# Causal layer: two projection jobs a batch, with the even and the odd features of all heads side by side in a bank

## The chip, the cores and the metric

The kernel runs on one core of a Trainium2 chip, in one launch. The metric is the device time of that core in microseconds (us). A core has five engines with a queue each: PE multiplies matrices, DVE (vector) and ACT (scalar) work on tiles, POOL (GpSimd) works on tiles in SBUF, and SP issues most DMAs here. PE writes its results to PSUM banks (512 floats per partition each); DVE and ACT read them there.

## The reference, cut to what matters

Two decoder layers run over x (16 batches, 256 rows, 256 features). The change touches the first sub-layer alone: causal self-attention with 16 heads of 16 features and a rotary embedding of q and k.

```
x = x + L0_attn(layernorm(x))                  # changed here; then cross attention,
                                               # a product-key FFN, band attention, a bidirectional
                                               # attention and a mixture of experts
L0_attn: k, q, v = split(x @ W_KQV.T, 3)       # 16 heads x 16 features
  rope:  xr, xi = x[..., ::2], x[..., 1::2]    # even and odd features of a head
         yr = xr*cos - xi*sin
         yi = xr*sin + xi*cos
  out = softmax(causal(rope(q) @ rope(k).T / 4)) @ v, then @ W_O.T
```

## The kernel before, in words

`attention_stage` is used three times (kinds causal, cross, band). The causal one works on 16 batches. `program` has a short lead-in (norm, turn, project and values for batches 0 and 1) and then calls `macro(e, b, par)` for each batch b. A macro is a list of 16 steps s, one per head, and every engine's queue is filled by walking the same list, so the order of work on an engine is the order of the calls in `macro`. At each step the engines handle three batches at once: `head(b, s)` computes the scores of batch b that go into the exponential, `find(b + 1, s)` computes scores of batch b + 1 whose row maximum DVE takes, and at chosen steps the work of batch b + 2 (`turn`, `project`, `stack`) and the end of batch b - 1 (`weigh`, `sums`, `sums_end`, `normalise`, `out`) is put in.

- `project(b + 2, j)` is a projection job. On PE it multiplies the transposed, normalised x with weights into bank (j + 1) % 2 of `ps_p`; the causal layer has weights wq and wk and copies of them with the two features of each pair swapped (wqs, wks), so that one bank holds q and its swapped form side by side. DVE multiplies the two halves with the cosine and sine tables into `rot`, and adds them twice, into `full` (float32) and into `part` (bfloat16). POOL then makes two more bfloat16 parts (middle and low) out of the remainder, with three instructions. SP writes the parts to DRAM scratch tensors (`qscratch`, `kscratch`), and `stack` reads them back, rearranged by head, into `qs` and `ks`.
- `find(h)` uses bank h % 2 of `ps_1`. PE may only write it when the maximum of head h - 2 has been taken, so it waits for `nmax_ready` to count h - 1 heads. DVE takes the two maxima of a head (row halves) with two TENSOR_REDUCE.
- `head(h)` uses `ps_2` in the same way with ACT's exponential (`p_ready`).
- `sums` and `sums_end` are two DVE reciprocals of 128 columns each; `normalise` on PE waits for the second of them (`rr_ready`). `norm(b + 3)` on DVE (s = 4) is two TENSOR_SCALAR from SBUF to SBUF. `moments` (s = 3) is two BN_STATS.
- `out(b - 1)` at s = 13 waits on PE for `proj_used` of all jobs of batch b + 2, because it writes bank 0 of `ps_p`.

In a table of what matters, the steps are these before the change:

| step s | calls that matter, in their order |
|---|---|
| 1 | turn |
| 2 | weigh (last quad of b - 1), project j = 0 |
| 3 | moments |
| 4 | sums, norm |
| 5 | sums_end, project j = 1 |
| 6 | weigh |
| 7 | normalise |
| 8 | stack, project j = 2 |
| 9 | turn_max |
| 10 | weigh |
| 11 | project j = 3 |
| 13, 15 | out; values |

The last call of each step (before turn_max) is `find(b + 1, s)`, and the first is `head(b, s)`.

## Time and profile before

| | us |
|---|---|
| median of 3 runs | 3635.33 (3632.45 to 3639.7) |
| the profiled execution's own time | 3634.44 |
| its span, first to last instruction | 3632.6 |

| engine | busy us over the span | share |
|---|---|---|
| PE | 3238.9 | 89% |
| DVE | 2620.0 | 72% |
| POOL | 2067.8 | 57% |
| ACT | 1834.9 | 51% |

The causal stage is the first 515.8 us or so: its last instruction on DVE (L880) starts at 515.1. In it the 16 macros run from about 67 to 515 us, and from the second to the fourteenth they repeat every 28.5 us. Busy shares are averages over stages with different limits, so what the change is worth is read from one macro.

### The profile page before, as it was taken

What the parts mean: (1) busy time and instruction counts of PE and PEld (TensorE: products, weight loads), DVE (VectorE), ACT (ScalarE), POOL (GpSimd) and SP (SyncE); (2) the same over time, 40 slices, a digit from 0 to 9 for tenths busy, and PEclk for the clock granted to TensorE, in tenths of its full rate; (3) what the DMA queues carried; (4) which work ended last, traced back from release to release, by engine and by line L of the source; (5) the groups of instructions that cost most, each with busy time, mean ns of one, the idle gap of its engine ahead of it and who ended that gap; (6) DMA issues with size and microseconds to landing.
All of it is one profiled execution on the core that took longest, in us unless ns stands there. A gap on an engine that the chain in (4) does not pass through costs nothing. (4 is left out here: it accounts for less than half of the span.)

```text
span 3632.6 us, 95157 instructions
## 1 busy us (share of the span) xinstructions
PE 3238.9 (89%) x33694; PEld 2753.6 (76%) x33695; DVE 2620.0 (72%) x10695; ACT 1834.9 (51%) x4800; POOL 2067.8 (57%) x2454
## 2 busy tenths in 40 slices
PE   5999977876599999999999999978888898899998
PEld 4777754554589999999999999855555686899998
DVE  6666634453899999999999999848888577333333
ACT  1434434543577777777777777726565221222221
POOL 4444435552377777777777777758886232333332
PEclk8999988997799999999999999989999898899999
DMA  5444424442200000000000000035553231566665
GB/s 155 111 118 125 109 66 119 122 116 74 84 2 2 2 2 2 2 2 2 3 2 2 2 3 2 2 82 128 138 131 88 84 100 44 170 185 177 186 176 134
DMA packets 255744, 277.73 MB, mean 76 GB/s; under 512 B 43871, under 2 KB 200287, under 8 KB 254815
## 3 DMA queue, kind: packets, MB, share of 16 engines
q1 hardware_dynamic: 241694, 253.40, 24.1%
q0 software_dynamic: 13632, 18.91, 3.6%
q8 instruction: 245, 4.01, 0.5%
q14 instruction: 173, 1.41, 0.1%
HBM read 187.34 MB, written 72.29 MB: 71 GB/s over the span
## 5 line engine op out<-in xcount | busy, mean ns | idle before, releaser
L1295 POOL TENSOR_TENSOR peer_hot_v<-peer_hot_e,peer_parts 80x512 bf16<-80x512 bf16 x768 | 920.9, 1226 | 271.0 <-DVE peer_hot_e L1338 266.2
L1091 PE MATMUL peer_ps_u<-peer_up,peer_g 128*128 128x256 f32 x2048 | 513.8, 396 | 0.6 <-DVE x_all L1438 0.6
L1072 PEld LDWEIGHTS peer_ps_h<-peer_xnT,peer_down 128*128 128x128 f32 x4096 | 503.9, 195 | 13.6 <-DMA peer_down<-in_peer_down 1.0
L1072 PE MATMUL peer_ps_h<-peer_xnT,peer_down 128*128 128x128 f32 x4096 | 505.9, 278 | 0.7 <-DMA peer_down<-in_peer_down 0.7
L1201 ACT ACTIVATE peer_hot_u<-peer_count,peer_minus_u 80x128 bf16<-80x128 bf16 x1536 | 462.3, 426 | 2.6 <-PE peer_ps_w L1082 1.5
L1082 PE MATMUL peer_ps_w<-peer_hot_v,peer_hot_u 80*128 80x32 bf16 x12288 | 348.3, 177 | 80.9 <-DVE peer_g L1352 36.1
L1091 PEld LDWEIGHTS peer_ps_u<-peer_up,peer_g 128*128 128x128 f32 x2048 | 382.5, 197 | 49.5 <-issue 1.0
L1082 PEld LDWEIGHTS peer_ps_w<-peer_hot_v,peer_hot_u 80*128 80x128 bf16 x12288 | 338.1, 97 | 101.2 <-issue 64.6
L2272 POOL DMA_INDIRECT out<-moe_y,moe_target x71 | 112.5, 1585 | 312.6 <-DVE moe_y L2371 309.6
L1169 ACT ACTIVATE peer_g<-peer_ps_h 128x512 f32<-128x512 f32 x256 | 145.3, 590 | 249.4 <-PE peer_ps_h L1072 249.1
L2216 PE MATMUL moe_ps_t<-moe_xgT,moe_w 128*128 128x128 f32 x2272 | 267.9, 277 | 0.0
L2216 PEld LDWEIGHTS moe_ps_t<-moe_xgT,moe_w 128*128 128x128 f32 x2272 | 262.0, 194 | 0.1
L2226 PE MATMUL moe_ps_y<-route_w,moe_hT 128*128 x1136 | 256.8, 379 | 0.0
L2226 PEld LDWEIGHTS moe_ps_y<-route_w,moe_hT 128*128 128x128 f32 x1136 | 210.5, 190 | 25.7
L1344 DVE TENSOR_TENSOR peer_hot_u<-peer_count,peer_uvT 80x2048 bf16<-80x2048 bf16 x160 | 229.9, 1437 | 0.0
L707 ACT ACTIVATE causal_probT<-causal_ps 128x384 f32<-128x384 f32 x256 | 124.5, 488 | 204.3 <-PE causal_ps L611 201.3
L2252 ACT ACTIVATE moe_hT<-moe_hT 128x512 f32<-128x512 f32 x142 | 89.4, 629 | 229.4 <-DVE moe_hT L2362 229.4
L843 DVE TENSOR_REDUCE band_nmax<-band_ps 128x2 f32<-128x512 f32 x256 | 171.6, 680 | 41.9 <-PE band_ps L584 41.3
L840 DVE TENSOR_REDUCE causal_nmax<-causal_ps 128x1 f32<-128x128 f32 (+1 forms) x512 | 153.0, 349 | 58.2 <-PE causal_ps L588 57.8
L1206 ACT ACTIVATE peer_hot_u<-peer_hot_u,peer_iota 80x2048 bf16<-80x2048 bf16 x96 | 192.2, 2002 | 3.1
L1352 DVE TENSOR_TENSOR peer_g<-peer_ps_w,peer_g 128x512 f32<-128x512 f32 x256 | 173.9, 679 | 11.8 <-PE peer_ps_w L1082 11.8
L707 ACT ACTIVATE band_probT<-band_ps 128x512 f32<-128x512 f32 x256 | 146.9, 593 | 64.2 <-PE band_ps L608 59.9
(373 smaller groups left out, 7235.0 us busy)
## 6 DMA issues: line engine op xcount, KB each, us to landing
moe_w<-in_moe_w SPq DMA_DIRECT2D x142, 512.0 KB, 4.5
causal_qs<-causal_qscratch SPq DMA_DIRECT2D x32, 384.0 KB, 3.9
cross_qs<-cross_qscratch SPq DMA_DIRECT2D x32, 384.0 KB, 3.6
band_qs<-band_qscratch SPq DMA_DIRECT2D x32, 384.0 KB, 4.0
route_w<-in_moe_w SPq DMA_DIRECT2D x8, 1024.0 KB, 6.0
causal_qscratch<-causal_part SPq DMA_DIRECT2D x32, 192.0 KB, 2.7
causal_kscratch<-causal_part SPq DMA_DIRECT2D x32, 192.0 KB, 2.0
causal_ks<-causal_kscratch SPq DMA_DIRECT2D x32, 192.0 KB, 4.2
```

The costliest lines, as they stand in the source:

```text
L707: nc.scalar.activation(probT[0:KN, h, :], ps_2[0:KN, h % 2, 0:COLS], ACT.Exp).then_inc(p_ready, 1)
L843: ins = nc.vector.tensor_reduce(nmax[:, :, h], ps_1[:, h % 2, 0:TT * KS].rearrange("p (q k) -> p q k", q=TT), AX.X, ALU.max, negate=True)
L1072: mm = nc.tensor.matmul(ps_h[:, n % 2, k * P:(k + 1) * P], down[:, c, 4 * n + k, :], xnT[:, par, c, :], start=(c == 0), stop=(c == DC - 1))
L1082: mm = nc.tensor.matmul(ps_w[:, n % 2, k * EV:(k + 1) * EV], hot_u[0:SEL, n % RING, k // 2, :, k % 2], hot_v[0:SEL, n % RING, part, k // 2 ...
L1091: mm = nc.tensor.matmul(ps_u[:], g[:, par, v, :], up[:, v, :], start=(v == 0), stop=(v == EV - 1))
L1201: ins = nc.scalar.activation(hot_u[0:SEL, n % RING, k // 2, :, k % 2], count[0:SEL, :, 0], ACT.Square, bias=minus_u[0:SEL, token:token + 1])
L1206: nc.scalar.activation(flat, flat, ACT.Relu, bias=iota[0:SEL, 1:2], scale=-1.0).then_inc(u_act_ready, 1)
L1295: ins = nc.gpsimd.tensor_tensor(hot_v[0:SEL, n % RING, part], hot_e[0:SEL, n % RING], w, ALU.mult)
L1344: nc.vector.tensor_tensor(hot_u[0:SEL, n % RING], numbers.broadcast_to((SEL, CHUNK // 2, P, 2)), ut, ALU.is_equal).then_inc(u_ready, 1)
L1352: nc.vector.tensor_tensor(gs, ps_w[:, n % 2, :].rearrange("p (k v) -> p v k", v=EV), gs, ALU.mult).then_inc(gw_ready, 1)
L2216: mm = nc.tensor.matmul(ps_h[:, half, m * P:(m + 1) * P], w1[:, par, half, c, m * P:(m + 1) * P], xgT[:, par, c, :], start=(c == 0), stop= ...
L2226: mm = nc.tensor.matmul(ps_y[:, par, 0:D], hT[:, par, m, :], w2[:, ex, m, :], start=(m == 0), stop=(m == HC - 1))
```

## The change

The weights wq and wk of the causal layer are reordered so that the 128 even features of all 16 heads come first and the 128 odd ones second. The swapped copies wqs and wks go away, with their loads. A bank now holds the even features in its first 256 columns and the odd ones in its second, for all heads, so that q is one job and k is another: `JOBS` has two entries in place of four, and they stand at steps 2 and 4 (before: 2, 5, 8, 11). Each job still has four matmuls of 128x256. On DVE a job is two multiplications of 512 columns and four additions or subtractions of 256 columns; on POOL it is three instructions of 512 columns. SP issues the same number of transfers of the same size, six for q together and two for k together. `rot` is now written whole by each job, `full` has a place for each job.

```diff
-    JOBS = [(qk, c) for c in range(DC) for qk in range(2)]
+    JOBS = [(0, 0), (1, 0)] if rope else [(qk, c) for c in range(DC) for qk in range(2)]
...
-    OUTS = 16 * (len(QRUNS) + 1)
+    OUTS = 16 * (len(QRUNS) + 1) * (DC if rope else 1)
...
-        PROJECT, OUT, VALUES, STACK = (2, 5, 8, 11), 13, 15, 8
+        PROJECT, OUT, VALUES, STACK = (2, 4) if rope else (2, 5, 8, 11), 13, 15, 8
...
# SP, stack: both halves of the heads now wait for all eight transfers
-                    sp.wait_ge(parts_out[c], OUTS * (b + 1))
+                    sp.wait_ge(parts_out[0 if rope else c], OUTS * (b + 1))
...
# PE, project
-                    mine = [("wq", "wqs"), ("wk", "wks")] if rope else [("wq",), ("wk",)]
-                    for k, name in enumerate(mine[qk]):
+                    name = ("wq", "wk")[qk]
+                    for k, chunk in enumerate(range(DC) if rope else (chunk,)):
...
# POOL, project
-                    nc.gpsimd.tensor_tensor(rest[:, 0:n], src, high, ALU.subtract)
-                    nc.gpsimd.tensor_tensor(part[:, j, 1, 0:n], src, high, ALU.subtract).then_inc(rest_ready, 1)
+                    nc.gpsimd.tensor_tensor(left, src, high, ALU.subtract)
+                    nc.gpsimd.tensor_tensor(middle, src, high, ALU.subtract).then_inc(rest_ready, 1)
...
# DVE, project
-                    wait(dve, proj_used, NJ * b + j - 1)
-                    nc.vector.tensor_tensor(rot[:, j % 2, 0, :], bank[:, 0:S], tab[cs][:], ALU.mult)
-                    steps.link(nc.vector.tensor_tensor(rot[:, j % 2, 1, :], bank[:, S:2 * S], tab[sn][:], ALU.mult))
...
+                    wait(dve, proj_used, NJ * b + j)
+                    nc.vector.tensor_tensor(by_cos, bank, cs, ALU.mult)
+                    steps.link(nc.vector.tensor_tensor(by_sin, bank, sn, ALU.mult))
...
-                    for dst in (full[:, j % 2, :], part[:, j, 0, :]):
-                        ins = nc.vector.tensor_tensor(dst, rot[:, j % 2, 0, :], rot[:, j % 2, 1, :], ALU.add)
+                    for dst in (full[:, j], part[:, DC * qk:DC * (qk + 1), 0, :]):
+                        nc.vector.tensor_tensor(dst[:, 0, :], by_cos[:, 0, :], by_sin[:, 1, :], ALU.subtract)
+                        ins = nc.vector.tensor_tensor(dst[:, 1, :], by_cos[:, 1, :], by_sin[:, 0, :], ALU.add)
```

How this moves instructions shows best on DVE and PE. First DVE in a steady macro, from `find` of step 2 on (TENSOR_REDUCE are the maxima of `find`, the two RECIPROCAL are `sums` and `sums_end`, `causal_xn` is `norm`, and `causal_rot`, `causal_full`, `causal_part` belong to the projection). Before:

```order
L840 TENSOR_REDUCE causal_nmax<-causal_ps 128x1 x2
L98 BN_STATS moments<-x_all 128x6 x2
L840 TENSOR_REDUCE causal_nmax<-causal_ps 128x1 x2
L861 RECIPROCAL causal_rr<-causal_ps_n 128x128
L802 TENSOR_SCALAR causal_xn<-x_all,mean,rstd 128x256 x2
L840 TENSOR_REDUCE causal_nmax<-causal_ps 128x1 x2
L864 RECIPROCAL causal_rr<-causal_ps_n 128x128
L815 TENSOR_TENSOR causal_rot<-causal_ps_p,causal_cosk 128x256
L816 TENSOR_TENSOR causal_rot<-causal_ps_p,causal_sink 128x256
L821 TENSOR_TENSOR causal_full<-causal_rot 128x256
L821 TENSOR_TENSOR causal_part<-causal_rot 128x256
L840 TENSOR_REDUCE causal_nmax<-causal_ps 128x1 x4
```

After the change, from the same place on (the line numbers are those of the changed kernel):

```order
L857 TENSOR_REDUCE causal_nmax<-causal_ps 128x1 x2
L98 BN_STATS moments<-x_all 128x6 x2
L857 TENSOR_REDUCE causal_nmax<-causal_ps 128x1 x2
L878 RECIPROCAL causal_rr<-causal_ps_n 128x128
L817 TENSOR_SCALAR causal_xn<-x_all,mean,rstd 128x256 x2
L831 TENSOR_TENSOR causal_rot<-causal_ps_p,causal_cosk 128x512
L832 TENSOR_TENSOR causal_rot<-causal_ps_p,causal_sink 128x512
L837 TENSOR_TENSOR causal_full<-causal_rot 128x256
L838 TENSOR_TENSOR causal_full<-causal_rot 128x256
L837 TENSOR_TENSOR causal_part<-causal_rot 128x256
L838 TENSOR_TENSOR causal_part<-causal_rot 128x256
L857 TENSOR_REDUCE causal_nmax<-causal_ps 128x1 x2
```

The second job stood behind the maxima of step 4 and behind the second reciprocal; it now stands ahead of both, right behind `norm`, and it is longer.

Then PE in the same macro, from `sums` at step 4 on (L584 and L588 are `find`, L608 and L611 are `head`, L628 is `weigh`). Before:

```order
L639 MATMUL causal_ps_n<-causal_oq,ahead_pack 32x256 x4
L584 MATMUL causal_ps<-causal_ks,causal_qs 128x128
L588 MATMUL causal_ps<-causal_mask,causal_ident 128x128
L584 MATMUL causal_ps<-causal_ks,causal_qs 128x256
L588 MATMUL causal_ps<-causal_mask,causal_ident 128x128
L608 MATMUL causal_ps<-causal_qs,causal_ks 128x256
L611 MATMUL causal_ps<-causal_mask,causal_ident 128x128
L608 MATMUL causal_ps<-causal_qs,causal_ks 128x128
L611 MATMUL causal_ps<-causal_mask,causal_ident 128x128
L558 MATMUL causal_ps_p<-causal_xnT,causal_wk 128x256 x2
L558 MATMUL causal_ps_p<-causal_xnT,causal_wks 128x256 x2
L584 MATMUL causal_ps<-causal_ks,causal_qs 128x128
```

After (L595 and L599 are `find`, L619 and L622 are `head`):

```order
L650 MATMUL causal_ps_n<-causal_oq,ahead_pack 32x256 x4
L569 MATMUL causal_ps_p<-causal_xnT,causal_wk 128x256 x4
L595 MATMUL causal_ps<-causal_ks,causal_qs 128x128
L599 MATMUL causal_ps<-causal_mask,causal_ident 128x128
L595 MATMUL causal_ps<-causal_ks,causal_qs 128x256
L599 MATMUL causal_ps<-causal_mask,causal_ident 128x128
L619 MATMUL causal_ps<-causal_qs,causal_ks 128x256
L622 MATMUL causal_ps<-causal_mask,causal_ident 128x128
L619 MATMUL causal_ps<-causal_qs,causal_ks 128x128
L622 MATMUL causal_ps<-causal_mask,causal_ident 128x128
L595 MATMUL causal_ps<-causal_ks,causal_qs 128x128
L599 MATMUL causal_ps<-causal_mask,causal_ident 128x128
```

The second job moved ahead of `find` of step 4 and uses wk alone; the jobs of steps 8 and 11 are gone from the queue.

## Rows read from the trace of the kernel before

**Rows 1.** Window of steady macros: PE, weight loads, DVE, ACT, POOL busy; clock; DMA.

```profile
95.02:465.85 370.83, 346.51 (x3403) 273.05 (x3404) 248.51 (x728) 151.28 (x354) 153.21 (x236) 1.00 0.45 117
```

**Rows 2.** Timeline of PE in one macro: start, us, instruction, [idle before].

```profile
238.98 1.13 PE L558 MATMUL causal_ps_p<-causal_xnT,causal_wq 128*128 128x256 f32 x4
...
243.15 0.23 PE L584 MATMUL causal_ps<-causal_ks,causal_qs 96*128 96x128 bf16 x1 [0.46 <-DVE causal_nmax L840]
...
246.97 0.23 PE L584 MATMUL causal_ps<-causal_ks,causal_qs 96*128 96x128 bf16 x1
...
254.37 1.08 PE L558 MATMUL causal_ps_p<-causal_xnT,causal_wk 128*128 128x256 f32 x4
...
256.15 0.22 PE L584 MATMUL causal_ps<-causal_ks,causal_qs 96*128 96x128 bf16 x1
...
256.72 0.22 PE L584 MATMUL causal_ps<-causal_ks,causal_qs 96*128 96x128 bf16 x1
...
258.03 1.97 PE L655 MATMUL causal_ps_p<-causal_wo,causal_onT 128*128 128x256 f32 x8 [0.57 <-issue]
```

**Rows 3.** Timeline of DVE in the same macro.

```profile
241.01 0.42 DVE L815 TENSOR_TENSOR causal_rot<-causal_ps_p,causal_cosq 128x256 f32<-128x256 f32 x1 [2.38 <-PE causal_ps_p L558]
...
241.80 0.43 DVE L821 TENSOR_TENSOR causal_full<-causal_rot 128x256 f32<-128x256 f32 x1
...
242.48 0.62 DVE L840 TENSOR_REDUCE causal_nmax<-causal_ps 128x1 f32<-128x128 f32 x2
243.01 0.74 DVE L98 BATCH_NORM_STATS2 moments<-x_all 128x6 f32<-128x256 f32 x2
...
244.19 0.95 DVE L861 RECIPROCAL causal_rr<-causal_ps_n 128x128 f32<-128x128 f32 x1
245.06 0.64 DVE L802 TENSOR_SCALAR causal_xn<-x_all,mean,rstd 128x256 f32<-128x256 f32 x2
245.61 0.62 DVE L840 TENSOR_REDUCE causal_nmax<-causal_ps 128x1 f32<-128x128 f32 x2
...
257.52 0.41 DVE L821 TENSOR_TENSOR causal_part<-causal_rot 128x256 bf16<-128x256 f32 x1
...
260.03 0.69 DVE L880 TENSOR_TENSOR x_all<-causal_ps_p,x_all 128x512 f32<-128x512 f32 x1 [1.04 <-PE causal_ps_p L655]
260.64 0.61 DVE L840 TENSOR_REDUCE causal_nmax<-causal_ps 128x1 f32<-128x128 f32 x2
```

**Rows 4.** POOL: one instruction of 256 columns, and all of 512 columns (min/median/max ns).

```profile
242.64 0.67 POOL L741 TENSOR_TENSOR causal_rest<-causal_full,causal_part 128x256 f32<-128x256 f32 x1 [3.19 <-DVE causal_part L821]
L763 POOL TENSOR_TENSOR x_all<-x_all,cross_bo x16: 1252/1258/1267, 524.4 to 830.8; 128x512 f32<-128x512 f32 x16
```

**Rows 5.** Timelines of DVE and of POOL in the lead-in, where both are busy.

```profile
38.12 1.56 DVE L802 TENSOR_SCALAR causal_xn<-x_all,mean,rstd 128x256 f32<-128x256 f32 x2
...
37.99 0.73 POOL L744 TENSOR_TENSOR causal_part<-causal_rest,causal_part 128x256 bf16<-128x256 f32 x1
38.87 0.67 POOL L741 TENSOR_TENSOR causal_rest<-causal_full,causal_part 128x256 f32<-128x256 f32 x1
```

**Rows 6.** PE after two idle gaps in the cross stage, and windows of 1 us there.

```profile
595.85 0.32 PE L608 MATMUL cross_ps<-cross_qs,cross_ks 99*120 99x256 bf16 x1 [1.77 <-DMA cross_qs<-cross_nscratch]
659.73 0.47 PE L608 MATMUL cross_ps<-cross_qs,cross_ks 99*120 99x256 bf16 x1 [4.22 <-DMA cross_qs<-cross_nscratch]
...
597.00:598.00 1.00, 1.00 (x10) 0.61 (x12) 0.41 (x1) 1.00 (x4) 0.82 (x2) 0.54 0.22 50
600.00:601.00 1.00, 1.00 (x8) 0.54 (x6) 0.18 (x1) 0.28 (x1) 0.43 (x1) 0.75 0.81 201
665.00:666.00 1.00, 1.00 (x12) 0.58 (x12) 0.25 (x1) 0.36 (x1) 0.00 (x0) 0.82 0.05 11
```

**Rows 7.** Timeline of SP's issues around the stack of one batch.

```profile
250.64 0.36 SPq L470 DMA_DIRECT2D causal_kscratch<-causal_part  x1
252.66 0.31 SPq L481 DMA_DIRECT2D causal_qs<-causal_qscratch  x1
```

More of the change, by code:

```diff
@@ L255, in attention_stage @@
         xnT = sb("xnT", [P, 2, DC, S])
-        full = sb("full", [P, 2, S])
-        rest = sb("rest", [P, S])
-        part = sb("part", [P, NJ, 3, S], BF16)
+        full = sb("full", [P, 2, DC, S] if rope else [P, 2, S])
+        rest = sb("rest", [P, DC, S] if rope else [P, S])
+        part = sb("part", [P, 2 * DC, 3, S], BF16)
         qs = sb("qs", [P, 2, HEADS, S], BF16)
@@ L464, in project @@
                     settle(split_ready, NJ * b + j + 1)
-                    if qk == 0:
+                    if rope:
+                        for odd in range(DC):
+                            mine = part[:, DC * qk + odd, :, :]
+                            if qk == 0:
+                                for slot, slots, a in QRUNS:
+                                    sp.dma_start(qscratch[par, slot:slot + slots, odd].rearrange("s p t -> p s t"),
+                                                 mine[:, a:a + 1, :].broadcast_to((P, slots, S))).then_inc(parts_out[0], 16)
+                            else:
+                                sp.dma_start(kscratch[par, :, odd].rearrange("s p t -> p s t"), mine).then_inc(parts_out[0], 16)
+                    elif qk == 0:
                         for slot, slots, a in QRUNS:
@@ L736, in project @@
                     n = S if qk == 0 else KS
-                    src, high = full[:, j % 2, 0:n], part[:, j, 0, 0:n]
+                    if rope:
+                        src, left = full[:, j], rest[:]
+                        high, middle, low = (part[:, DC * qk:DC * (qk + 1), k, :] for k in range(3))
+                    else:
+                        src, left = full[:, j % 2, 0:n], rest[:, 0:n]
+                        high, middle, low = (part[:, j, k, 0:n] for k in range(3))
                     pool.wait_ge(proj_used, NJ * b + j + 1)
                     wait(pool, split_ready, NJ * b + j)
-                    nc.gpsimd.tensor_tensor(rest[:, 0:n], src, high, ALU.subtract)
-                    nc.gpsimd.tensor_tensor(part[:, j, 1, 0:n], src, high, ALU.subtract).then_inc(rest_ready, 1)
+                    nc.gpsimd.tensor_tensor(left, src, high, ALU.subtract)
+                    nc.gpsimd.tensor_tensor(middle, src, high, ALU.subtract).then_inc(rest_ready, 1)
                     pool.wait_ge(rest_ready, NJ * b + j + 1)
-                    nc.gpsimd.tensor_tensor(part[:, j, 2, 0:n], rest[:, 0:n], part[:, j, 1, 0:n],
-                                            ALU.subtract).then_inc(split_ready, 1)
+                    nc.gpsimd.tensor_tensor(low, left, middle, ALU.subtract).then_inc(split_ready, 1)
                 def factor(self, b, par, h):
@@ L810, in project @@
                     qk, c = JOBS[j]
[L811 to L816 removed]
+                    bank = ps_p[:, (j + 1) % 2, :].rearrange("p (o t) -> p o t", o=DC)
+                    cs, sn = (tab[n][:].unsqueeze(1).broadcast_to((P, DC, S)) for n in (("cosk", "sink") if qk else ("cosq", "sinq")))
+                    by_cos, by_sin = rot[:, 0], rot[:, 1]
+                    wait(dve, proj_used, NJ * b + j)
+                    nc.vector.tensor_tensor(by_cos, bank, cs, ALU.mult)
+                    steps.link(nc.vector.tensor_tensor(by_sin, bank, sn, ALU.mult))
                     wait(dve, split_ready, NJ * b + j - 1)
[L819 to L821 removed]
+                    wait(dve, parts_out[0], OUTS * b)
+                    for dst in (full[:, j], part[:, DC * qk:DC * (qk + 1), 0, :]):
+                        nc.vector.tensor_tensor(dst[:, 0, :], by_cos[:, 0, :], by_sin[:, 1, :], ALU.subtract)
+                        ins = nc.vector.tensor_tensor(dst[:, 1, :], by_cos[:, 1, :], by_sin[:, 0, :], ALU.add)
                     ins.then_inc(proj_used, 1)
@@ L2383, in _chunk_bias, with _even_first @@
     return _rows_first(np, b).reshape(DC, P).T
-def _pairs_swapped(wt):
-    return wt.reshape(wt.shape[0], -1, 2)[:, :, ::-1].reshape(wt.shape)
+def _even_first(np, wt):
+    return wt.reshape(wt.shape[0], HEADS, HD // 2, 2).transpose(0, 3, 2, 1).reshape(wt.shape)
 def _constants(np):
```

28 lines of the change are left out of this document (11 added, 17 removed).

## The prediction

> **What bounds the kernel now.** I read first the window table over the causal stage's steady macros: in 370.8 us PE is busy for 346.5 us (93%), DVE for 248.5 us (67%), POOL for 153.2 us, and PE's granted clock is 1.00, its upper level of 2.4 GHz [rows 1]. By these sums PE is the bound and DVE has room. But both are sums over a macro, and the change packs work into three of its sixteen steps, so I then read one macro instruction by instruction on PE and DVE, and asked at each place which wait ends last. PE waits three times in that macro for DVE. One is plain: `find` of step 4 starts at 243.15 after 0.46 us idle, because the maxima of step 2 started on DVE at 242.48, took 0.62 us and let PE go 0.05 us later; so a `find` starts no sooner than 0.67 us after the start of the maxima two heads back [rows 2, 3]. One is hidden under the word issue: `out` starts at 258.03 after 0.57 us idle, and DVE's last addition of job 3 ends at 257.52 + 0.41 = 257.93, 0.10 us earlier, and `out` waits for just that job [rows 2, 3]. (The third, at `turn_max` of step 0, doesn't touch the change.)
>
> **What the change removes on PE.** A job keeps its length: four matmuls, 256.15 - 254.37 = 1.78 us on the path [rows 2]. The jobs of steps 8 and 11 go: 3.56 us a macro. They stood on PE's own path, so this is a real gain as long as PE stays the bound. The wait before `out` goes too (0.57 us), since the last job is now done by step 7. Together -4.13 us a macro.
>
> **What it does to DVE.** A job before lasts 242.48 - 241.01 = 1.47 us, of which the two additions are 0.68 us and the two multiplications 0.79 us [rows 3]. After it has two multiplications of 512 columns and four additions of 256. A 512-column operation out of PSUM takes 260.64 - 260.03 = 0.61 us from start to start [rows 3]; two of them and 0.11 us for the result of the last to arrive (the 0.45 us from the second multiplication to the first addition before against the 0.34 us of an unlinked one, my reading of 0.79 - 0.34) are 1.33 us, four additions 1.36 us, so a job is 2.69 us. Twice 2.69 is less than four times 1.47: over the macro DVE gains 0.5 us. What counts is where they stand.
>
> I count from the start of the first job on PE, which is 238.98 [rows 2]. DVE starts on it 2.03 us later [rows 3]. Its queue from there to the maxima of step 4 is: job 0 (2.69), maxima of step 2 (0.53), moments and maxima of step 3 (244.19 - 243.01 = 1.18), the first reciprocal (0.87), `norm` (N), job 1 (2.69). Then 0.67 us until PE may start `find` of step 6, which needs the maxima of step 4. The sum is 2.03 + 7.96 + N + 0.67 = 10.66 + N.
>
> N is `norm`, 245.61 - 245.06 = 0.55 us where POOL is idle [rows 3]. But POOL will not be idle: its part of job 0 begins 0.1 us after DVE's end, thus at 4.8 us, and its instructions grow from 0.67 us to 1.26 us [rows 4], so it is busy until about 8.7 us; `norm` comes at 7.3 us, before POOL's third instruction. In the lead-in the same pair of TENSOR_SCALAR took 1.56 us while POOL worked: the first started at 38.12 under POOL's instruction of 37.99, the second had to let 38.87 pass [rows 5]. So each of the two waits until a POOL instruction is over. With 1.26 us ones the first slips in at about 7.3 us, the second waits for the third POOL instruction (7.6 to 8.9 us), and N is about 1.9 us. The Trainium skill (SBUF — State Buffer, Who interferes with whom) says the same of `tensor_scalar` in a two-port mode: the two engines share a port pair, it is locked for a whole instruction, and the other one fully blocks; by that rule the longer POOL instruction is the price, not the longer DVE one, and the trace agrees (1.56 us).
>
> So `find` of step 6 starts at 11.2 us (N free) or 12.5 us (N blocked); before it was at 246.97 - 238.98 = 7.99 us [rows 2]. That is 3.2 or 4.5 us later, and PE idles for nearly all of it, since everything in its queue behind `find` of step 6 (head 7, `normalise`, and so on) waits with it. From `find` of step 6 to that of step 12 PE took 256.72 - 246.97 = 9.75 us [rows 2], now 3.56 us less. (`normalise` waits 0.3 us for the second reciprocal, which stands behind the late maxima, and `find` of step 9 another 0.3 us; the wait before step 7 that they replace was as long.) Per macro, at full clock: 3.2 - 4.13 = -0.9 us, or 4.5 - 4.13 = +0.4 us. I take the second.
>
> **The clock.** PE has had no idle gap over 0.6 us in a macro so far. Now it has one of about 4.5 us. In the cross stage a gap of 1.77 us is followed by a granted clock of 0.54 in the window 597 to 598 and 0.75 in 600 to 601: some 3.4 us at the lower level, 1.2 GHz, though PE was busy throughout. After a gap of 4.22 us the first matmul already takes 0.47 us where the other took 0.32 us, and the full clock is back only in the window 665 to 666 (0.82), 5.6 us after 659.73 [rows 6]. So 3.4 to 5.6 us of PE's work at half speed per macro, half of which is lost: 1.7 to 2.8 us, less the 0.6 us of waits which a slower PE no longer meets. I take 1.6 us (1.0 to 2.2). The Trainium skill (TensorE: Matmul & The Clock Gate, Why this matters for your kernels) warns of idle gaps between bursts of matmuls for this reason, and that speaks against this change; the trace agrees (0.47 us against 0.32 us).
>
> **POOL, SP, loads.** POOL: three times 1.26 us against six times 0.67 us, no more in sum. SP issues the same transfers, but `stack` of step 8 now needs both jobs. DVE's job 1 ends at about 11.9 us, POOL's part at 15.7 us, two issues take 0.8 us, and the transfer 2.0 us from issue to the `stack` that waits for it (252.66 - 250.64) [rows 7]: `stack` goes out at 18.5 us in place of 13.7 us, and behind it in SP's queue `turn_max` of step 9, with a transfer out and one back of such 2 us each. Both are needed at step 0 of the next macro, which begins after `out` (19.05 us) and the four jobs of PE behind it, 5 us and more later. I cost it at nothing; without that cover each us costs a us a macro. The two loads that go away end before DVE has its first `norm`, so nothing there. The values job and `turn` are unchanged.
>
> **The sum.** Macros 1 to 12 have all of this: 12 x (0.4 + 1.6) = +24 us. Macro 0 has no reciprocals and no `out`, but also no 0.57 us to win: about +2. Macro 13 has no `norm`, so its `find` of step 6 comes 1.9 us sooner: about -0.5. Macros 14 and 15 project nothing. The lead-in has four short DVE jobs in a row per batch, now two long ones (-0.5 us a batch) whose additions and `norm` meet longer POOL instructions: -1 us (-3.5 if nothing blocks). In all +24.5 us on the profiled execution's own 3634.4 us, which is 0.9 us under the median of the runs shown. I predict 3660 us.
>
> **The rivals.**
> - Gap but no loss of clock (the dip is as rare as between the short gaps of today): 12 x 0.4 + 1 - 1 - 1.4 = +3, 3638 us. For it: the causal macros with gaps of 0.5 us never lose the clock. Against: [rows 6]. Chance 0.10.
> - `norm` doesn't meet POOL, the clock falls all the same after 3.2 us: 12 x (-0.9 + 1.5) - 3.5 = +4, 3639 us. Against: [rows 5]. Chance 0.10.
> - The other side: PE's 4.13 us come through. That needs DVE's queue to end before PE asks for it. One place decides it: job 1 ahead of the maxima of step 4. If the stall there were under 4.13 us and the clock stayed (N free, no dip), the stage gains 0.9 x 12 + 3.5 + 1 = 15 us, 3620 us; with no stall it would be 13 x 4.1 = 53 us, 3581 us. For it: DVE is busy only 67%. Against: DVE is in order, and 7.96 us of named instructions stand there. The break-even stall is 4.1 us with full clock, 2.5 us with the dip. Chance 0.12, nearly all of it for the small gain.
> - A second wait: the slow clock lasts beyond step 12, or `stack` and `turn_max` arrive late at step 0. With 2 us more a macro: +50 us, 3685 us. Chance 0.08.
>
> **How the numbers follow.** The forecast itself has 0.60; its own range is 12 x (1.4 to 2.6) - 2 to + 3, thus 3649 to 3669 us. For 8 in 10 I go down to 3632 us, which takes in the first two rivals, and up to 3678 us, part of the last. A measurement of this kernel tells 0.2% (7.3 us) from no change. Faster: 0.12, from the third rival. Same: the first two and a sliver of the forecast, 0.22. Slower: 0.66.
>
> **What would show it.** In the changed kernel's timeline of PE: a gap of 4 to 5 us before `find` of step 6 put down to `causal_nmax`, in each of the macros 1 to 12; on DVE job 0 of 2.7 us, `norm` of about 1.9 us under POOL, and job 1 of 2.7 us right behind it; granted clock well under 1.00 in the steady windows, in stretches after the gap; no gap before `out`; a period of about 30.5 us where it is 28.5 now. The prediction is wrong if the gap is under 2.5 us (job or `norm` shorter than my terms), or if the clock stays at 1.00.

## The result, and the profile after

The changed kernel takes 3661.31 us (median of 4 runs, 3652.51 to 3666.35), the kernel before 3636.97 us (4 runs, 3632.45 to 3639.7): a ratio of 1.0066, with a 95% interval of 1.005 to 1.0081. That is 24 us slower, where +24.5 us were forecast.

The window table over the steady macros of the changed kernel (us; busy time of PE, weight loads, DVE, ACT, POOL; granted clock; DMA share; GB/s) answers to [rows 1]:

```profile
98.20:487.10 388.90, 327.50 (x3181) 256.20 (x3178) 254.70 (x673) 150.43 (x351) 139.41 (x156) 0.90 0.41 110
```

PE does less (327.5 us in place of 346.5 us) in a longer time, and its clock is no longer 1.00. So read who PE waits for (in the same window: us in total, times, longest):

```profile
PE causal_ps L595 <- DVE causal_nmax L857: 55.7, 27, 4.2
PE causal_ps_n L609 <- DVE causal_nmax L857: 5.5, 13, 0.4
```

There is one wait of weight, of `find` for the maxima, and one per macro is over 2 us. PE's timeline of one macro shows where:

```profile
248.10 1.99 PE L569 MATMUL causal_ps_p<-causal_xnT,causal_wq 128*128 128x256 f32 x8
...
251.74 1.99 PE L569 MATMUL causal_ps_p<-causal_xnT,causal_wk 128*128 128x256 f32 x8
...
254.65 0.23 PE L595 MATMUL causal_ps<-causal_ks,causal_qs 96*128 96x128 bf16 x1 [0.35 <-DVE causal_nmax L857]
254.78 0.27 PE L595 MATMUL causal_ps<-causal_ks,causal_qs 96*128 96x256 bf16 x1
...
260.19 0.29 PE L595 MATMUL causal_ps<-causal_ks,causal_qs 96*128 96x128 bf16 x1 [4.00 <-DVE causal_nmax L857]
260.38 0.42 PE L595 MATMUL causal_ps<-causal_ks,causal_qs 96*128 96x256 bf16 x1
```

(The trace lists each of a job's four matmuls twice.) `find` of step 6 stands 4.00 us idle, 12.09 us after the start of job 0. DVE never stops in that time:

```profile
250.13 0.69 DVE L831 TENSOR_TENSOR causal_rot<-causal_ps_p,causal_cosq 128x512 f32<-128x512 f32 x1 [2.38 <-PE causal_ps_p L569]
...
252.80 0.61 DVE L857 TENSOR_REDUCE causal_nmax<-causal_ps 128x1 f32<-128x128 f32 x2
...
255.38 1.56 DVE L817 TENSOR_SCALAR causal_xn<-x_all,mean,rstd 128x256 f32<-128x256 f32 x2
256.86 0.68 DVE L831 TENSOR_TENSOR causal_rot<-causal_ps_p,causal_cosk 128x512 f32<-128x512 f32 x1
...
259.52 0.61 DVE L857 TENSOR_REDUCE causal_nmax<-causal_ps 128x1 f32<-128x128 f32 x2
```

A job is 2.67 us (250.13 to 252.80, 256.86 to 259.52 is 2.66), and `norm` 1.48 us from start to start (0.55 us before [rows 3]). Its first instruction starts 0.07 us behind POOL's third one and is held until that one ends at 256.47:

```profile
255.31 1.16 POOL L760 TENSOR_TENSOR causal_part<-causal_rest,causal_part 128x512 bf16<-128x512 f32 x1
```

The windows of 1 us in the same macro (same columns as above) show the clock: it falls while PE idles and stays at 0.50, the lower level of 1.2 GHz, for five microseconds of work after that. In the timeline above the matmul of 256 columns behind the gap takes 0.42 us; its like in the same macro, ahead of the gap, takes 0.27 us.

```profile
257.00:258.00 1.00, 0.00 (x0) 0.00 (x0) 1.00 (x2) 0.00 (x0) 0.00 (x0) 1.00 0.62 188
258.00:259.00 1.00, 0.00 (x0) 0.00 (x0) 0.97 (x4) 0.00 (x0) 0.00 (x0) 0.86 0.70 208
...
261.00:262.00 1.00, 1.00 (x6) 0.91 (x5) 0.99 (x4) 0.49 (x1) 0.94 (x1) 0.50 0.85 262
...
265.00:266.00 1.00, 1.00 (x12) 0.91 (x11) 0.67 (x3) 0.49 (x1) 0.00 (x0) 0.73 0.33 97
```

Last, SP's issues, which answer to [rows 7]: `stack` leaves 17.70 us after job 0's start, and PE doesn't wait for a transfer in this macro.

```profile
263.20 0.90 SPq L473 DMA_DIRECT2D causal_kscratch<-causal_part  x2
265.80 0.33 SPq L492 DMA_DIRECT2D causal_qs<-causal_qscratch  x1
...
271.08 0.24 SPq L502 DMA_DIRECT2D causal_qs<-causal_nscratch  x1
```

The start of the first multiplication of job 0 on DVE is a good mark for a whole macro. In the kernel before it falls at 72.93 (macro 0), 98.92 (macro 1) and 440.70 us (macro 13), in the changed one at 71.82, 100.30 and 460.90 us. By these marks, in the two profiled executions:

| part | before | after | difference |
|---|---|---|---|
| lead-in, to macro 0 | 72.93 | 71.82 | -1.1 |
| macro 0 | 25.99 | 28.48 | +2.5 |
| macros 1 to 12, each | 28.48 | 30.05 | 12 x 1.57 = +18.8 |
| macro 13 to the stage's last instruction on DVE (L880, now L897) | 74.44 | 74.43 | 0.0 |
| the causal stage | | | +20.2 |
| everything after it, to the span's end | | | +4.4 |

### The profile page after: what moved, and what is told of

Its sections match the earlier page's. It is cut to its first block and busy times, and to the rows that moved or that the text cites. A ratio compares the mean times of both kernels' runs of the same rounds, so it can differ in the third digit from the quotient of the medians.

```text
span 3657.2 us, 94356 instructions
## 1 busy us (share of the span) xinstructions
PE 3210.0 (88%) x33438; PEld 2728.0 (75%) x33439; DVE 2624.0 (72%) x10631; ACT 1837.9 (50%) x4800; POOL 2051.8 (56%) x2358
```

## The experiments

Each kernel is the changed one with the edit shown, unless said otherwise. The kernel before was run anew beside every group of experiments (medians of 3634.97 to 3638.56 us), and each ratio goes by the runs of its own group; so a difference of microseconds between two groups can be off by some 3 us. "Period" is the mean distance of the marks above over macros 1 to 12, from the profiled execution; "last" is the start of the causal stage's last instruction on DVE.

| kernel | us, median (range, runs) | ratio to before (95%) | period | clock in 110 to 480 us | last |
|---|---|---|---|---|---|
| before | | | 28.48 | 1.00 | 515.1 |
| changed | 3661.31 (3652.51 to 3666.35, 4) | 1.0066 (1.005 to 1.0081) | 30.05 | 0.90 | 535.3 |
| e1 norm at step 12 | 3633.72 (3625.84 to 3639.57, 10) | 0.9985 (0.9976 to 0.9995) | 28.32 | 0.93 | 510.3 |
| e2 filler in the gap | 3642.33 (3636.27 to 3651.15, 10) | 1.0021 (1.0011 to 1.0031) | 28.90 | 1.00 | 522.6 |
| e3 second job at 6 | 3686.49 (3681.48 to 3688.51, 4) | 1.0137 (1.012 to 1.0154) | 31.97 | 0.88 | 564.9 |
| e4 the same, norm late | 3691.19 (3688.91 to 3693.21, 4) | 1.0153 (1.0136 to 1.017) | 32.12 | 0.88 | 566.0 |
| e5 light work between | 3629.27 (3622.65 to 3642.67, 10) | 0.998 (0.9964 to 0.9996) | 28.11 | 0.93 | 508.9 |
| e6 the same, jobs at 1, 3 | 3641.26 (3636.79 to 3645.92, 10) | 1.0008 (0.9999 to 1.0018) | 28.78 | 0.93 | 518.0 |
| e7 before, jobs at 2 to 5 | 3635.72 (3628.26 to 3640.32, 10) | 0.9989 (0.9979 to 0.9998) | 28.31 | 1.00 | 513.5 |
| e8 as e4, turn_max first | 3665.5 (3663.04 to 3670.27, 4) | 1.0071 (1.0052 to 1.009) | 30.65 | 0.90 | 546.6 |
| e9 as e5, filler | 3617.7 (3613.27 to 3624.84, 6) | 0.9955 (0.9943 to 0.9967) | 26.97 | 0.99 | 493.3 |
| e10 as e5, POOL after both | 3680.24 (3675.77 to 3681.84, 4) | 1.0119 (1.0104 to 1.0133) | 30.83 | 0.93 | 556.0 |
| e11 as e5, POOL's third after both | 3633.87 (3627.69 to 3643.5, 12) | 1.0001 (0.9992 to 1.0009) | 28.63 | 0.94 | 515.2 |
| e12 as e11, turn_max first | 3617.93 (3610.46 to 3631.64, 12) | 0.9956 (0.994 to 0.9973) | 27.55 | 0.98 | 498.3 |

### e1: norm out of POOL's way

```diff
-        WEIGH, SUMS, NORMALISE, MOMENTS, NORM = 6, 4, 7, 3, 4
+        WEIGH, SUMS, NORMALISE, MOMENTS, NORM = 6, 4, 7, 3, 12 if rope else 4
```

> The changed kernel with norm moved from step 4 to step 12 in the causal layer. Theory of the prediction (PE idles before find of step 6 for as long as DVE's queue of step 2 to 4 lasts; norm under POOL is 1.48 us of it): the gap before that find falls from 4.0 us to 2.5 us in every macro, and the steady period from 30.1 us to 28.6 us if the clock still dips after it, to about 27 us if it doesn't; in all 20 to 39 us less than the changed kernel, 3622 to 3641 us. Rival (norm is hidden, the gap is set by something else): gap 4.0 us, 3660 us.

The gap before `find` of step 6 is 2.47 us and the time falls by 0.8%, in the range expected. Moving two instructions of DVE gives all of the loss back, and a little more: 30.05 - 28.32 = 1.73 us a macro, of which 4.00 - 2.47 = 1.53 us is the gap. PE's timeline, and windows of 1 us, of e1:

```profile
247.41 0.29 PE L595 MATMUL causal_ps<-causal_ks,causal_qs 96*128 96x128 bf16 x1 [2.47 <-DVE causal_nmax L857]
```

```profile
247.00:248.00 1.00, 0.59 (x5) 0.53 (x6) 1.00 (x3) 0.00 (x0) 1.00 (x1) 0.59 0.66 196
...
250.00:251.00 1.00, 1.00 (x11) 0.70 (x9) 0.39 (x1) 0.00 (x0) 0.40 (x1) 0.71 0.78 266
```

The clock still falls after a gap of 2.47 us, for more than three microseconds. It does so behind all 12 gaps of this length, but behind the one of 2.68 us in macro 1 (before 104.86) it stays at 1.00.

### e2: PE kept busy in the gap

```diff
+                    if rope and h == 6 and 1 <= b < B - 1:
+                        pe.wait_ge(proj_used, NJ * (b + 1) + 1)
+                        for k in range(8):
+                            nc.tensor.matmul(ps_p[:, 1, 0:S], w["wv"][:, 0, 0:P], w["wo"][:, 0, :],
+                                             start=True, stop=True)
```

The eight matmuls stand in `find`, into a bank that is free then; nothing reads their result.

> The changed kernel with eight extra matmuls of 128x256 (float32, 3.5 us at full clock) into bank 1 of ps_p ahead of find of step 6, whose result is overwritten and used by nobody: they fill the gap of 4.0 us and end before DVE lets PE go. Theory (half of the loss is the clock falling after the gap): granted clock 1.00 in the steady macros, find 6 to find 12 takes 6.2 to 6.4 us in place of 8.0 us, period 28.5 us in place of 30.1 us, about 19 to 21 us less, 3640 us. Rival (the clock costs nothing because PE then waits for DVE anyway): period and time as in the changed kernel, 3660 us, in spite of the clock at 1.00.

It came out at 3642.33 us. DVE sets the end of the gap, so the filler can't make it shorter; all that it changes is the clock. PE's timeline and the window table of e2:

```profile
248.35 3.72 PE L594 MATMUL causal_ps_p<-causal_wo,causal_wv 128*128 128x256 f32 x16
...
252.43 0.23 PE L600 MATMUL causal_ps<-causal_ks,causal_qs 96*128 96x128 bf16 x1 [0.36 <-DVE causal_nmax L862]
```

```profile
110.00:480.00 370.00, 345.50 (x3367) 269.94 (x3364) 249.12 (x665) 149.22 (x349) 135.54 (x153) 1.00 0.42 114
```

From mark to mark the undisturbed macros take 28.40 us (185.57, 213.97, 242.37, 270.76), and the changed kernel 30.05 us: the slow clock alone costs 1.65 us a macro. The changed kernel's own macros agree: three of the 12 have the low clock for some 3 us and take 29.55 us on average, nine have it for over 6 us and take 30.22 us; that is 1.15 and 1.82 us over the 28.40 us. The mean of e2 is 28.90 us because PE waited six times, 6.8 us in all, for the read back of the maxima at step 0. Useless work of PE in the gap makes the kernel faster by 19 us (16 us by the two ratios).

### e3, e4 and e8: the second job further back

e3 moves only the second job, e4 also `norm` and `stack`, and e8 is e4 with `stack` one step later still, so that `turn_max` of step 9 goes out ahead of it in SP's queue.

```diff
# e3
-        PROJECT, OUT, VALUES, STACK = (2, 4) if rope else (2, 5, 8, 11), 13, 15, 8
+        PROJECT, OUT, VALUES, STACK = (2, 6) if rope else (2, 5, 8, 11), 13, 15, 8
# e4
+        PROJECT, OUT, VALUES, STACK = (2, 6) if rope else (2, 5, 8, 11), 13, 15, 9 if rope else 8
+        WEIGH, SUMS, NORMALISE, MOMENTS, NORM = 6, 4, 7, 3, 12 if rope else 4
# e8, over e4
+        PROJECT, OUT, VALUES, STACK = (2, 6) if rope else (2, 5, 8, 11), 13, 15, 10 if rope else 8
```

> The changed kernel with the second job at step 6 in place of 4; all else as it is. Theory (it is the place, not the merged job): the one gap of 4.0 us becomes two, about 1.3 us before find of step 6 and 2.2 us before find of step 8, the clock dips less, period 27.3 to 28.8 us, 3625 to 3644 us, about the kernel before. Rival (the merged job itself is dear wherever it stands): period 30 us, 3655 us or more.

> Second job at step 6, norm at step 12, stack of the first half of the heads at step 9. By the rows DVE then has about 10.4 us of work in steps 2 to 7 and PE about 10.1 us, so no gap is over 1.5 us, the clock stays at 1.00, and PE's 3.56 us a macro come through: period 24.7 us, 3590 us (3585 to 3610). Rival (a later wait takes the place of the gap: stack needs both jobs, and POOL, two transfers and a read stand between the second job and find of step 0): a wait for causal_qs or causal_ks at step 0, period 27 us and more, 3620 us and more.

> The kernel of e4 with stack of the first half at step 10, behind turn_max of step 9 in SP's queue. Theory (in e4 PE waited at step 0 for qs from nscratch, as turn_max stood in SP's queue behind stack, which waits for both jobs): that wait goes, and one for causal_ks or causal_qs from the scratch tensors takes its place at find of step 0, because stack is later by the time of turn_max; the period stays within 1 us of e4, 3680 to 3700 us. Rival (the order in SP's queue alone is the fault): period 2 us less, 3660 us.

Both e3 and e4 missed badly, on the other side: 3686.49 and 3691.19 us. Each came out on the side of its rival (in e3, the merged job is dear wherever it stands, 3655 us or more; in e4, a later wait takes the gap's place, 3620 us and more), and both rivals have a part in it. Moving `norm` out of the way brings nothing here: PE waits 44.5 us for the maxima in e3 and 44.9 us in e4. In the waits of PE (e4, 98 to 480 us) two causes stand side by side:

```profile
PE causal_ps L595 <- DVE causal_nmax L857: 44.9, 47, 1.7
PE causal_ps L619 <- DMA causal_qs<-causal_nscratch: 19.0, 11, 3.0
```

The second is the transfer of the maxima, late at step 0. SP's timeline of e4 shows it behind `stack`, which itself waits for the writes of the second job:

```profile
275.81 0.90 SPq L473 DMA_DIRECT2D causal_kscratch<-causal_part  x2
278.40 0.33 SPq L492 DMA_DIRECT2D causal_qs<-causal_qscratch  x1
...
280.23 0.28 SPq L500 DMA_DIRECT2D causal_nscratch<-causal_npart  x1
283.69 0.24 SPq L502 DMA_DIRECT2D causal_qs<-causal_nscratch  x1
```

The write of the maxima stood in line. e8 tests that, in the waits of PE (98 to 480 us):

```profile
PE causal_ps L595 <- DVE causal_nmax L857: 47.0, 49, 1.7
PE causal_ps L595 <- DMA causal_ks<-causal_kscratch: 5.3, 5, 1.4
```

The wait for `causal_qs` is gone, 5.3 us of waits for `causal_ks` are all that is left of transfers, and the time falls by 26 us (30 us by the two ratios), nearly to the rival's 3660 us and against what I held for likelier.

The first cause stays in e8. I put the rest of its loss against e1 (30.65 against 28.32 us a macro) down to it and to the clock behind it (0.90 against 0.93); no run takes the two apart. Where the jobs stand apart, each has its own stall: DVE begins 2.03 us after PE's start, needs 2.67 us, and `find` follows 0.67 us after the start of the maxima, 5.4 us in all. PE has 3.7 us of work in that time (the job and two steps), and stands for 1.67 us (263.27 in e4's timeline, before `find` of step 4), then 0.44, 1.41 and 0.31 us. In the changed kernel the first of these is only 0.35 us, since PE fills it with the second job. So the packing of the jobs close together is not wrong in itself.

### e7: the old jobs, as densely packed

This is the kernel before with its four jobs at steps 2 to 5.

```diff
-        PROJECT, OUT, VALUES, STACK = (2, 5, 8, 11), 13, 15, 8
+        PROJECT, OUT, VALUES, STACK = (2, 3, 4, 5) if rope else (2, 5, 8, 11), 13, 15, 8
```

> The kernel before with its four jobs at steps 2, 3, 4, 5 and nothing merged. Theory (the gap comes from PE running out of work while DVE is still at the job: PE lost half of its matmuls there, DVE did not lose its work): PE still has four jobs of 1.78 us in steps 2 to 5, arrives at find of step 6 some 11 us after the first job's start, when DVE lets it go, so gaps stay under 1.5 us each, clock 1.00, period 28.5 to 29.5 us, 3632 to 3650 us. Rival (dense placement alone is the fault): a gap of 3 us and more with a dip of the clock, 3655 us and more.

As expected: gaps of 0.81 and 0.31 us, clock 1.00, period 28.31 us. Short jobs with short POOL instructions can be packed closely without a loss, so the placement alone is not what costs 4 us.

### e5 and e6: other work between the jobs

```diff
-        WEIGH, SUMS, NORMALISE, MOMENTS, NORM = 6, 4, 7, 3, 4
+        WEIGH, SUMS, NORMALISE, MOMENTS, NORM = (6, 5, 8, 10, 12) if rope else (6, 4, 7, 3, 4)
# e6 also
-        PROJECT, OUT, VALUES, STACK = (2, 4) if rope else (2, 5, 8, 11), 13, 15, 8
+        PROJECT, OUT, VALUES, STACK = (1, 3) if rope else (2, 5, 8, 11), 13, 15, 8
-                    if s == 1:
+                    if s == (0 if rope else 1):
                         e.turn(b + 2, par)
```

> The changed kernel, jobs at steps 2 and 4 as it is, with DVE's other work taken out of their way in the causal layer: norm at step 12, moments at 10, the reciprocals at 5 and 6, normalise at 8. Theory (the gap before find of step 6 is the sum of what stands in DVE's queue): the gap falls from 4.0 us by 1.48 (norm), 0.65 (moments) and 0.87 (first reciprocal) to 1.0 us and the clock stays at 1.00, so PE alone would allow a period of 24.9 us. But the chain through both jobs, POOL, the transfers out and back and turn_max in SP's queue then takes until about 23 us after the first job's start, where head 0 comes at 21.3 us: a wait for causal_qs of 1 to 2 us at step 0, period 25 to 27 us, 3590 to 3617 us. Rival (the gap is not a sum, each merged job costs PE its own stall of 1.5 us wherever it stands, as in the runs with the second job at 6): period 28 us, 3630 us.

> The kernel of e5 with turn at step 0 and the jobs at steps 1 and 3. If the wait at step 0 for the chain through SP is what holds e5 back, one step (about 1.5 us) of it goes: period 25 to 26 us, 10 to 20 us less than e5, 3580 to 3605 us. If e5 is held by DVE alone: the same time as e5.

With moments, reciprocals and `norm` all moved away, DVE has only job 0, the maxima of steps 2 and 3, and job 1 in its queue. e5 is the fastest up to here, but only by 0.2%, and missed its range: the time is where the rival had it (3630 us), and the gap is 1.91 us and not 1.0 us. PE, DVE and POOL of e5 show that the rival's reason, a stall of 1.5 us for each job, is not the right one, for PE stands just 0.45 us at step 4:

```profile
246.49 0.23 PE L595 MATMUL causal_ps<-causal_ks,causal_qs 96*128 96x128 bf16 x1 [1.91 <-DVE causal_nmax L857]
```

```profile
243.51 0.43 DVE L837 TENSOR_TENSOR causal_full<-causal_rot 128x256 f32<-128x256 f32 x1
243.85 1.38 DVE L838 TENSOR_TENSOR causal_full<-causal_rot 128x256 f32<-128x256 f32 x1
245.16 0.41 DVE L837 TENSOR_TENSOR causal_part<-causal_rot 128x256 bf16<-128x256 f32 x1
```

```profile
242.41 1.16 POOL L758 TENSOR_TENSOR causal_part<-causal_full,causal_part 128x512 bf16<-128x512 f32 x1
243.65 1.30 POOL L760 TENSOR_TENSOR causal_part<-causal_rest,causal_part 128x512 bf16<-128x512 f32 x1
```

One addition of DVE takes 1.31 us from start to start where it takes 0.34 us elsewhere, and ends at 245.23, 0.28 us behind POOL's instruction (244.95), as if it ran only then. Taking `norm` out of DVE's queue moved job 1 forward, into POOL's three instructions. e6 is slower by 12 us and fits neither of its expectations: `weigh`, 0.8 us of PE's work, no longer stands ahead of the gap, which is 2.62 us then, the addition is as long (1.38 us), and PE waits 12.9 us in all, ten times, for ACT's exponentials.

### e9: how much of e5 is the clock

e9 is e5 with four matmuls ahead of `find` of step 6, written as in e2.

```diff
+                        for k in range(4):
```

> The kernel with weigh, sums, normalise and norm between the two jobs, and in the macros 1 to 14 four matmuls of 128x256 in float32 (about 1.8 us) into a spare bank right before find of step 6, where PE otherwise waits 1.9 us. They compute nothing that is used. Theory (what is left of the loss after the gap of 1.9 us is the low clock that follows it, since DVE sets the end of the gap and PE's own work behind it then runs at full speed): the gap before find of step 6 is under 0.4 us, the clock 1.00 in nearly all macros, the period 26.3 to 26.8 us instead of 28.06, and the time 13 x 1.3 to 1.7 us below the kernel without the filler: 3605 to 3615 us. Rival (the low clock costs nothing there, because another chain, such as the transfers of stack and turn_max, sets the period): the gap goes, a wait for qs or ks appears at step 0 in its place, and the time stays at 3625 to 3632 us.

3617.7 us is 2.7 us over the range expected, and the ratio of 0.9955 (0.9943 to 0.9967) beside e5's 0.998 (0.9964 to 0.9996) gives 9 us. The gap before step 6 is gone, 0.45 and 0.59 us are left, no transfer takes its place (2.2 us over three waits), and the period falls by 1.14 us, where 1.3 to 1.7 us were expected. The clock costs less after the short gap than after the long one (1.65 us in e2): in e5 it is low for some 3 us in ten of 13 macros and for over 6 us in three, in the changed kernel for some 3 us in three of 12 and for over 6 us in nine.

### e10, e11 and e12: the lock and the queue

In e10 POOL takes up job 0 only when DVE is done with both jobs. In e11 only its third instruction of job 0 waits so. e12 is e11 with `stack` behind `turn_max`. All three stand on e5's edit.

```diff
# e10
-                    pool.wait_ge(proj_used, NJ * b + j + 1)
+                    pool.wait_ge(proj_used, NJ * b + (2 if rope else j + 1))
# e11 and e12
                     pool.wait_ge(rest_ready, NJ * b + j + 1)
+                    if rope:
+                        pool.wait_ge(proj_used, NJ * b + 2)
                     nc.gpsimd.tensor_tensor(low, left, middle, ALU.subtract).then_inc(split_ready, 1)
# e12
-        PROJECT, OUT, VALUES, STACK = (2, 4) if rope else (2, 5, 8, 11), 13, 15, 8
+        PROJECT, OUT, VALUES, STACK = (2, 4) if rope else (2, 5, 8, 11), 13, 15, 10 if rope else 8
```

> The kernel with weigh, sums, normalise and norm between the two jobs, but POOL takes up its part of job 0 only when DVE is done with both jobs of the batch. Theory (the last addition of job 1 took 1.3 us instead of 0.34 us because an instruction of POOL was under way): all four additions of job 1 take 0.34 us from start to start, the gap before find of step 6 falls from 1.9 to about 0.95 us, the clock falls in few of the macros, and the period is 26.4 to 27.2 us; POOL's six instructions end some 3 us later, and stack with them, which may cost up to 0.5 us a macro at step 0. 3603 to 3622 us. Rival (the addition is long for another reason, or the delay of POOL costs what it brings): the gap stays at 1.9 us, or a wait for qs at step 0 takes its place, and the time is 3625 to 3640 us.

> The kernel with weigh, sums, normalise and norm between the two jobs; POOL starts its part of job 0 at once as there, and only its third instruction of job 0 waits until DVE is done with both jobs. Theory (one instruction of POOL under way costs DVE's job 1 0.97 us; the stall of 0.95 us that is left lets the clock stand, as it did where POOL waited with all of job 0; and since POOL's later work moves by only some 0.1 us, stack isn't late): gap before find of step 6 about 0.95 us, clock 1.00 in nearly all macros, no wait for a transfer at step 0, period 28.06 - 0.97 - 1.1 = 26.0 us, and a time of 3596 to 3610 us. Rival (the chain from POOL over stack to step 0 had no slack at all, or another instruction of POOL meets job 1): a wait for qs at step 0, or an addition of over 1 us, and 3615 to 3630 us.

> The kernel in which POOL's third instruction of job 0 waits for DVE's second job, with stack moved from step 8 to step 10, so that in SP's queue turn_max (the write and the read back of the maxima) goes out ahead of it and not behind it. Theory (what gave the gain back was qs<-nscratch, queued behind a stack that came late): the wait for qs<-nscratch at step 0, 22.3 us in all over eleven macros, is gone; the gaps of 0.95, 0.59 and 0.45 us stay, clock 1.00 in nearly all macros, period 26.0 to 26.6 us, time 3600 to 3612 us. Rival (both transfers need the same time from POOL's end, whatever their order): a wait for ks<-kscratch at find of step 0 of 1.5 us or more takes its place, and the time is 3620 to 3636 us.

The theory of the lock (POOL under way holds up the addition) held to the row. First all instructions of that line that write `causal_full` in e5, of job 0 and of job 1 (min, median, max in ns), then the same in e10:

```profile
L838 DVE TENSOR_TENSOR causal_full<-causal_rot x26: 417/901/1386, 99.2 to 440.3; 128x256 f32<-128x256 f32 x26
```

```profile
L838 DVE TENSOR_TENSOR causal_full<-causal_rot x25: 417/418/419, 108.6 to 478.7; 128x256 f32<-128x256 f32 x25
```

With POOL silent none of them is long, and the gap before step 6 is the 0.95 us forecast. PE's timeline and windows of e10:

```profile
254.69 0.28 PE L619 MATMUL causal_ps<-causal_qs,causal_ks 99*128 99x256 bf16 x1 [3.26 <-DMA causal_qs<-causal_nscratch]
...
268.34 0.23 PE L595 MATMUL causal_ps<-causal_ks,causal_qs 96*128 96x128 bf16 x1 [0.95 <-DVE causal_nmax L857]
```

```profile
257.00:258.00 1.00, 1.00 (x9) 0.73 (x7) 0.37 (x2) 0.60 (x1) 0.92 (x2) 0.50 1.02 209
...
270.00:271.00 1.00, 0.88 (x8) 0.67 (x7) 1.00 (x4) 0.49 (x1) 0.92 (x2) 1.00 0.00 0
```

After this gap of 0.95 us the clock stays at 1.00, as in ten of 13 macros; in three (gaps before 114.03, 175.45 and 236.89) it falls to 0.50 for some 3 us. But the other row of the timeline shows the price: POOL is done with the batch 2.7 us later, `stack` goes out 17.3 us after the mark (13.6 us in e5), and behind it in SP's queue the maxima. PE waits 42.5 us for them in twelve macros, and the clock falls at that place instead (0.50 in the first of the windows). I had put at most 0.5 us a macro on it; it costs more than all that was won, 3680.24 us. That is what the rival said in its second half, and 40 us beyond its range. In the macro of the mark 261.28 `stack` is 3.7 us later than in e5, PE reaches `head` of step 0 1.9 us sooner (20.6 us after the mark, 22.5 us in e5) and waits 3.8 us, so e5's cover was about 1.8 us.

e11 delays one instruction, and POOL's last one ends 11.4 us after the mark (11.0 us in e5). Still PE waits for the same transfer. The waits of PE (98 to 480 us) of e11, then of e12:

```profile
PE causal_ps L595 <- DVE causal_nmax L859: 25.9, 39, 0.9
PE causal_ps L619 <- DMA causal_qs<-causal_nscratch: 22.3, 11, 3.0
```

```profile
PE causal_ps L595 <- DVE causal_nmax L859: 25.9, 39, 0.9
PE causal_ps L595 <- DMA causal_ks<-causal_kscratch: 11.1, 12, 1.8
...
PE causal_ps L619 <- DMA causal_qs<-causal_nscratch: 0.9, 1, 0.9
```

What was won at step 6 is lost at step 0, and e11 is where the kernel before is (1.0001). In six of 13 macros `stack` leaves 3.5 to 3.9 us after SP's last issue of the second job's writes (in the other seven 1.7 to 2.5 us), in e5 1.70 us after it in every one, and after those six PE waits 2.6 to 3.0 us at step 0. Macros without it take 27.0 us from mark to mark (157.12 to 184.16, 215.16 to 242.20), the others up to 31.1 us. Why the same writes are confirmed some 2 us later there is open. SP issues them 0.60 us behind those of q, where it is 1.48 us in e5, but that isn't enough as a reason: the seven macros without the delay have the same 0.60 us, and in e1, with 2.1 us between the two, `stack` leaves up to 3.0 us after the last issue in five of the macros 2 to 12.

The short gap isn't safe for the clock here either. In four of 13 macros of e11 it falls behind a gap of 0.94 or 0.95 us, as in the second of the two macros of 27.0 us just named:

```profile
222.22 0.23 PE L595 MATMUL causal_ps<-causal_ks,causal_qs 96*128 96x128 bf16 x1 [0.94 <-DVE causal_nmax L859]
```

```profile
224.00:225.00 1.00, 1.00 (x7) 0.83 (x5) 1.00 (x5) 0.30 (x1) 1.00 (x2) 0.50 1.03 308
```

e12 takes the maxima out from behind `stack`. The wait for them is nearly gone (22.3 to 0.9 us), and 11.1 us of waits for `causal_ks` stand in its place: theory and rival each in part, 3617.93 us, 6 us above the range of the one and 2 us below that of the other. It is level with e9 as the fastest kernel here, 0.44% under the kernel before, and without a useless matmul.

## Why the prediction was right, point by point

- **DVE's queue ahead of find of step 6** was the mechanism, in every one of the macros 1 to 12. It starts 12.09 us after job 0 (12.5 forecast), and PE idles 4.00 us (about 4.5). Jobs: 2.67 us each (2.69). Start of DVE behind PE: 2.03 us, to the hundredth.
- **Norm blocked by POOL**: 1.48 us (1.9, and 0.55 unblocked). The step held; the size was off because a POOL instruction of 512 columns is 1.16 us with these types and not the 1.26 us of [rows 4]. So POOL's third one ran from 7.21 to 8.37 us after job 0's start where I had 7.6 to 8.9 us; it held the first instruction of the pair and not the second, and let both go sooner. That 0.42 us is nearly the whole of the error in the 12.5 us. e1 confirms it: with `norm` away the gap is 1.53 us smaller.
- **PE's gain** of 4.13 us a macro was real. At full clock (e2's undisturbed macros) the period is 28.40 us, before 28.48 us: gap and gain cancel, where I had +0.4 us, and the difference is again `norm`.
- **The clock**: 1.6 us forecast, 1.65 us by e2. From `find` of step 6 to that of step 12 PE takes 8.01 us (7.8 forecast, 6.26 at full clock in e2). The forecast took it that the clock falls behind every gap of this size, from two rows of the cross stage. It did, in all 12 macros, but the trace of before also has a gap that speaks against a plain rule, and I had not read it. "No idle gap over 0.6 us in a macro" is wrong for the macros at the two ends. In macro 14 PE idles 2.04 us and the clock stays at 1.00:

```profile
474.72 0.28 PE L608 MATMUL causal_ps<-causal_qs,causal_ks 99*128 99x256 bf16 x1 [2.04 <-ACT causal_probT L707]
```

```profile
475.00:476.00 1.00, 0.99 (x14) 0.72 (x10) 0.97 (x5) 0.64 (x3) 0.00 (x0) 1.00 0.00 0
```

- **Stack and turn_max at no cost** held in the macros 1 to 13: `stack` went out at 17.7 us (18.5), and PE waits for no transfer. It failed in macro 0, at whose end (step 0 of macro 1) PE waits 2.39 us for `causal_qs<-causal_nscratch`. I had +2 us for that macro from DVE and got +2.5 us. And the cover of "5 us and more" holds only for a PE as slow as this one: in e5, two microseconds a macro faster, it was 1.8 us.
- **The sum**: 12 x 1.57 = 18.8 us in place of 12 x 2.0 = 24; macro 0 +2.5 (+2), lead-in -1.1 (-1), the end 0.0 (-0.5). The stage loses 20.2 us, where 24.5 us were forecast. The profiled execution is 24.6 us longer, because the stages behind it took 4.4 us more in it. Their code is the same, and in the other profiled executions here they differ from the kernel before by between -7 and +8 us (e11: 515.2 against 515.1 us at the stage's end, yet 6.7 us less span). That the total came within 2 us is thus in part luck; the stage's term was 4.3 us too large.
- **The rivals**: the clock fell, so the first is out, and e2 shows what it would have been: 3642 us, 3638 forecast. `norm` was blocked, so the second is out, and e1, with `norm` moved away altogether, is near what it would have been: 3634 us, 3639 forecast. PE's gain came through best in e9 and e12, and even there just 17 us of the 53 us (by their ratios e5 is 7 us and e1 5 us under the kernel before). The second wait, the fourth rival, is what e3, e4, e10 and e11 ran into.

## What to carry to other kernels

Fewer, longer instructions on a helper engine are not cheaper if the bound engine waits for what stands behind them in that engine's queue: add up the queue between two results that the bound engine asks for, not the busy time. When the gap is removed, look at once at what ran in its shade; here the loss went from `norm` to an addition that POOL held up, and from there to a transfer that stood behind another in SP's queue. Two stalls that PE can fill with each other's work (jobs close together) beat the same two apart.
